# Column loops moved behind the first gathers in the projection and attention stages of a two-layer graph network

## The reference

```
h = relu(layernorm(x))
x = x + GCN(h):      h1 = batchnorm(h @ w1.T + b1); y = (relu(h1) @ w2.T + b2) @ w_gcn.T
                     deg = edges per dst, with one more self loop; dinv = deg ** -0.5
                     out[d] = sum over edges (y[s] * dinv[s]) * dinv[d] + b_gcn
h = relu(layernorm(x))
x = x + attention(h): q, k, v = h @ Wq + bq, h @ Wk + bk, h @ Wv + bv     (8 heads of 32)
                     s[e] = q[row] . k[col] * scale; softmax over the edges of each row
                     out[row] = (sum of a[e] * v[col]) @ Wo + bo
```

## Time and profile before

| what | value |
|---|---|
| median of 3 runs | 3371.53 us |
| the profiled execution's own time | 3372.14 us |
| its span, first to last instruction | 3370.4 us |
| busy: PE, DVE, ACT, POOL | 92%, 83%, 74%, 58% |
| granted TensorE clock, mean | 0.97 of full |
| end of the node stage's last DVE instruction | 1132.55 us |
| projection stage, first ACT instruction | 1132.84 us |
| projection stage, last ACT instruction | ends 2279.35 us |
| attention stage, first ACT instruction | 2282.27 us |

### The profile page before, as it was taken

The page is one execution under the profiler, slowest core; times in us unless marked ns, Lnnn a source line. Parts: engine busy times, 40 slices in busy tenths (PEclk is TensorE's granted clock), DMA queues, the critical chain, the costliest instruction groups (busy, mean ns, idle before and its releaser), DMA issues. The chain is left out here.

```text
span 3370.4 us, 80751 instructions
## 1 busy us (share of the span) xinstructions
PE 3093.8 (92%) x20244; PEld 2504.8 (74%) x20244; DVE 2804.0 (83%) x7375; ACT 2501.4 (74%) x7073; POOL 1953.4 (58%) x1668
## 2 busy tenths in 40 slices
PE   4899998899998399999999999994999999999999
PEld 2455554677776288888888888883999999999998
DVE  8888887778886478888888888885888888888887
ACT  3788887699997577777777777753777777777776
POOL 1155553255554387777777777754555555555553
PEclk7999999899999699999999999996999999999999
DMA  3455554788887578888888888865777777777774
GB/s 103 166 203 202 204 201 173 244 303 305 311 305 249 212 278 311 306 313 307 308 307 311 309 308 310 308 238 191 243 257 256 253 255 252 253 252 253 253 255 155
DMA packets 335634, 861.27 MB, mean 256 GB/s; under 512 B 98484, under 2 KB 152923, under 8 KB 323019
## 3 DMA queue, kind: packets, MB, share of 16 engines
q1 hardware_dynamic: 239178, 677.96, 56.4%
q0 software_dynamic: 66256, 78.94, 8.1%
q10 hardware_dynamic: 30128, 103.56, 7.7%
HBM read 521.95 MB, written 416.52 MB: 278 GB/s over the span
## 5 line engine op out<-in xcount | busy, mean ns | idle before, releaser
L1879 PE MATMUL c_qkv_ps<-w_qkv_hi,c_ht_hi 128*128 128x256 f16 x2352 | 642.3, 273 | 0.0
L1879 PE MATMUL c_qkv_ps<-w_qkv_lo,c_ht_hi 128*128 128x256 f16 x2352 | 642.3, 273 | 0.0
L1879 PE MATMUL c_qkv_ps<-w_qkv_hi,c_ht_lo 128*128 128x256 f16 x2352 | 642.2, 273 | 0.0
L2312 ACT ACTIVATE e_mine<-e_mine,e_attention 128x32 f32<-128x32 f32 x2352 | 518.7, 308 | 70.6 <-DVE e_attention L2546 70.6
L2259 POOL DMA_INDIRECT e_kv<-kv_table,e_near x392 | 401.7, 1025 | 113.4 <-issue 103.1
L1749 POOL DMA_INDIRECT c_got<-y_table,c_near x392 | 395.1, 1008 | 108.5 <-issue 97.5
L596 POOL DMA_INDIRECT dst_slots<-dst_word,dst_goal x240 | 241.4, 1006 | 302.7 <-ACT a_hn L660 237.5
L2348 PE MATMUL e_out_ps<-w_out,e_mean_t 128*128 128x256 f32 x1568 | 392.8, 380 | 0.0
L2251 POOL TENSOR_TENSOR e_kv<-e_kv,e_part_of 128x1024 f32<-128x1024 f32 x98 | 186.9, 1908 | 344.5 <-DVE e_part_of L2581 344.5
L722 PE MATMUL a_h_ps<-a_ht,w_t 128*128 128x512 f32 x784 | 363.1, 607 | 17.8 <-ACT h L642 14.1
L1513 POOL DMA_INDIRECT src_slots<-staged_word,staged_goal x240 | 234.9, 979 | 243.4 <-DVE sort_lane_hot L1402 170.9
(11 more groups left out here) (432 smaller groups left out, 7669.3 us busy)
## 6 DMA issues: line engine op xcount, KB each, us to landing
kv_table<-c_kv SPq DMA_DIRECT2D x98, 1024.0 KB
h_table<-h ACTq DMA_DIRECT2D x98, 512.0 KB, 2.7
h<-h_table SPq DMA_DIRECT2D x98, 512.0 KB, 4.1
y_table<-y_out ACTq DMA_DIRECT2D x98, 512.0 KB
agg_table<-agg_out SPq DMA_DIRECT2D x98, 512.0 KB
c_agg<-agg_table SPq DMA_DIRECT2D x98, 512.0 KB, 4.8
x_table<-c_x SPq DMA_DIRECT2D x98, 512.0 KB, 2.7
q_table<-c_q SPq DMA_DIRECT2D x98, 512.0 KB
```

Of the source, the lines that this page charges most:

```text
L1879: last = nc.tensor.matmul(qkv_ps[n][:, j * D:(j + 1) * D], h[u][:, kc, j * P:(j + 1) * P], wt[:, kc, n * D:(n + 1) * D], start=m == 0, sto ...
L2312: last = nc.scalar.activation(of_head, of_head, ACT.Copy, scale=attention[u][:, j, h, 0:1])
```

## The change

Six things, all in how stages start:

1. Projection stage: the column's word is decoded, and its gather issued, for turn 0 ahead of the loop; the loop body follows on each engine behind the first tiles' gathers (at the turn of the first sums), decodes the next word and issues the next gather at its end. `found` is one column wider for this. On POOL: gathers of tile 0, the column's gather, gathers of tile 1, the loop, gathers of tile 2.
2. SP no longer waits for the number of columns but for `sum_settled` (1 if nothing is unsorted), so the loads of `agg` start without the loop.
3. Gathers of the projection stage name partitions 0 to 126 only; POOL doesn't wait for the bias rows any more, each of the first four gathers waits for its own buffer's clearing, and SP's bias loads follow each clearing.
4. `absent` is made in the projection stage, on DVE, behind the sums of tile 1. `has_self` starts in the node stage, and `no_self` too, by a subtraction on POOL; POOL has no other `tensor_tensor` ahead of the projection stage.
5. Attention stage: the loop's first decoding stands at the end of the projection stage on DVE; on POOL the column's four gathers come first, then those of tiles 0, 1 and 2, then the loop's body with the scatters, the wait for them and four more gathers of a next column; on PE, ACT and DVE the body stands ahead of turn 1. SP copies to and from spare tiles behind the tables (`agg_spare`, `kv_spare`) when nothing is slow, doesn't wait for the columns then (`slow_settled`), and POOL doesn't wait for the second copy.
6. All six kv buffers are cleared by ACT, each ahead of its first index tile.

The core of the diff (the bodies of both loops are the same instructions as before, but for the decoding at their end):

```diff
+def is_first(t):
+    return t is not None and isinstance(t[0], int) and t[0] == 0 and t[1] == 0
...
-    agg_table = dram("agg_table", [TAB + 2 * P, D])
+    agg_spare = dram("agg_spare", [TAB + 2 * TILE, D])
+    agg_table = agg_spare[0:TAB + 2 * P, :]
-    kv_table = dram("kv_table", [TAB, 2 * D])
+    kv_spare = dram("kv_spare", [TAB + 2 * TILE, 2 * D])
+    kv_table = kv_spare[0:TAB, :]
...
+ v.tensor_scalar(has_self[:, :], n_self[:, :], 1.0, None, ALU.min).then_inc(has_ready, 1)
...
+ v.tensor_scalar(slow_last[:, :], slow[:, :], float(-2 * TILE), float((NT + 1) * TILE), ALU.mult, ALU.add)
- for l in range(LAYERS):
-     v.tensor_scalar(absent[:, :, l], own_degree[:, :], float(l), LOW, ALU.is_le, ALU.mult)
...
+ pool.wait_ge(has_ready, 1)
+ nc.gpsimd.tensor_tensor(no_self[:, :], has_self[:, :], one_col[:, 0:1].to_broadcast([P, NT * ROWS]), ALU.subtract)
...   (projection stage, SP)
- sp.wait_ge(got_cleared, 4)
  for w in four:
+     sp.wait_ge(got_cleared, w + 1)
- hold(sp, column_free, columns + 1)
+ hold(sp, column_free, settled)
...   (projection stage, POOL)
- with pool.Fori(0, columns) as n:
-     hold(pool, staged, n + 1)
-     gather(one_got[:, :], y_table, from_i[:, 0:1]).then_inc(gathered, 16)
-     hold(pool, summed_ready, n + 1)
-     hold(pool, goal_ready, n + 1)
-     scatter(agg_table, goal[:, 0:1], one_summed[:, :], compute_op=ALU.add).then_inc(scattered, 16)
-     hold(pool, scattered, n * 16 + 16)
-     pool.sem_inc(column_free, 1)
- pool.wait_ge(bias_rows, 64)
+ def add_columns():
+     with pool.Fori(0, columns) as n:
+         hold(pool, summed_ready, n + 1)
+         hold(pool, goal_ready, n + 1)
+         scatter(agg_table, goal[:, 0:1], one_summed[:, :], compute_op=ALU.add).then_inc(scattered, 16)
+         hold(pool, scattered, n * 16 + 16)
+         pool.sem_inc(column_free, 1)
+         hold(pool, staged, n + 2)
+         gather_column()
  def step(at):
+     if is_first(at(3)):
+         add_columns()
...
-     nc.gpsimd.indirect_dma_start(out=got[w][:, j, :], out_offset=None, in_=y_table,
-                                  in_offset=bass.IndirectOffsetOnAxis(ap=near[w][:, j:j + 1], axis=0),
+     nc.gpsimd.indirect_dma_start(out=got[w][0:P - 1, j, :], out_offset=None, in_=y_table,
+                                  in_offset=bass.IndirectOffsetOnAxis(ap=near[w][0:P - 1, j:j + 1], axis=0),
+     if is_first(at(1)):
+         pool.wait_ge(staged, 1)
+         gather_column()
...   (projection stage, DVE, end of a step, then end of the stage)
+ if at(3) is not None and isinstance(at(3)[0], int) and tile_of(at(3)) == 1:
+     for l in range(LAYERS):
+         v.tensor_scalar(absent[:, :, l], own_degree[:, :], float(l), LOW, ALU.is_le, ALU.mult)
  over_tiles(dve, plan, 9, step, slots=4)
+ decode_slow(dve, 0)
+ stage_slow()
...   (attention stage, SP)
- hold(sp, gathered, columns * 64)
  for t in range(SHORT):
      sp.dma_start(flat(q[t][:, :, :]), row_block(q_table, t)).then_inc(q_loaded[t], 16)
- hold(sp, column_free, columns + 1)
+ hold(sp, copied, tiles * 16)
+ hold(sp, column_free, settled)
- sp.sem_inc(rows_settled, 1)
...   (attention stage, POOL)
- pool.wait_ge(rows_settled, 1)
- pool.wait_ge(kv_cleared, RING)
+ pool.wait_ge(s_staged, 1)
+ gather_column()
...
+ if isinstance(t, int) and t < RING:
+     pool.wait_ge(kv_cleared, t + 1)
...
+ if is_first(at(0)):
+     settle_columns()
...   (attention stage, ACT, ahead of each of the first six index tiles)
+ if isinstance(t, int) and t < RING:
+     nc.scalar.activation(kv[w][:, :, :].rearrange("p r d -> p (r d)"), one_col[:, 0:1].to_broadcast([P, ROWS * 2 * D]),
+                          ACT.Copy, scale=0.0).then_inc(kv_cleared, 1)
```

More of the change, by code:

```diff
@@ L310, in build @@
         sum_cols = sb("sum_cols", [P, 1], I32, where=early)
+        sum_settled = sb("sum_settled", [P, 1], I32, where=early)
         sum_lane = sb("sum_lane", [P, NT * ROWS], where=early)
@@ L315, in build @@
         own_degree = sb("own_degree", [P, NT * ROWS], where=early)
+        has_self = sb("has_self", [P, NT * ROWS], where=early)
+        no_self = sb("no_self", [P, NT * ROWS], where=early)
         mid = ExitStack()
@@ L1483, in _ @@
                     v.tensor_copy(sum_cols[:, :], over[:, 3:4])
+                    v.tensor_scalar(sum_settled[:, :], over[:, 3:4], unsorted[:, 0:1], 1.0, ALU.mult, ALU.add)
                     v.tensor_scalar(sum_lane[:, :], slots_f[:, 0, :], neg_one[:, 0:1], float(P), ALU.mult, ALU.add)
@@ L1561, in build, with stage_slow @@
+        def stage_slow():
+            v = nc.vector
+            v.tensor_tensor(s_ends[:, 0:1], s_keys[:, 0:1], s_back[:, :], ALU.add)
+            v.tensor_copy(s_ends[:, 1:2], s_keys[:, 1:2]).then_inc(s_staged, 1)
         with ExitStack() as part, nc.Block() as block:
@@ L1609, in build @@
             state = [sb(f"c_state{u}", [P, ROWS, STATE], where=part) for u in two]
-            has_self = sb("has_self", [P, NT * ROWS], where=part)
-            no_self = sb("no_self", [P, NT * ROWS], where=part)
             got_cleared = sem("c_got_cleared")
@@ L1904, in _, with decode @@
                 v = nc.vector
-                with dve.Fori(0, columns) as n:
+                def decode(n):
                     steps = 8
@@ L1930, in _, with stage @@
                     link(v.scalar_tensor_tensor(node[:, :], odd[:, :], -254.0, node[:, :], ALU.mult, ALU.add))
+                    assert done[0] == steps
+                def stage(n):
+                    if not isinstance(n, int):
+                        hold(dve, gathered, n * 16)
                     v.scalar_tensor_tensor(from_i[:, :], node[:, :], parts[:, 1:2], live[:, :], ALU.add, ALU.mult).then_inc(staged, 1)
-                    assert done[0] == steps
-                    dve.wait_ge(across_ready, n + 1)
@@ L1941, in _, with rank_columns @@
-                    dve.wait_ge(ranked, n * 2 + 2)
-                    v.tensor_scalar(goal[:, :], apart[:, :], spare[:, 2:3], None, ALU.add).then_inc(goal_ready, 1)
-                v.tensor_scalar(has_self[:, :], n_self[:, :], 1.0, None, ALU.min).then_inc(c_chain, 1)
-                dve.wait_ge(c_chain, 1)
-                v.tensor_scalar(no_self[:, :], has_self[:, :], -1.0, -LOW, ALU.add, ALU.mult).then_inc(c_chain, 1)
-                dve.wait_ge(c_chain, 2)
+                def rank_columns():
+                    with dve.Fori(0, columns) as n:
+                        dve.wait_ge(across_ready, n + 1)
+                        v.tensor_scalar(same[:, :], across[:, 0:P], key[:, 0:1], None, ALU.is_equal)
+                        v.scalar_tensor_tensor(rank_of[:, :], across[:, 0:P], key[:, 0:1], earlier[:, :], ALU.is_equal, ALU.mult,
+                                               accum_out=rank[:, 0:1])
+                        v.tensor_scalar(apart[:, :], key[:, :], spare[:, 2:3], None, ALU.subtract).then_inc(ranked, 1)
+                        dve.wait_ge(ranked, n * 2 + 1)
+                        v.scalar_tensor_tensor(apart[:, :], rank[:, :], 0.0, apart[:, :], ALU.is_equal, ALU.mult).then_inc(ranked, 1)
+                        dve.wait_ge(ranked, n * 2 + 2)
+                        hold(dve, column_free, n + 1)
+                        v.tensor_scalar(goal[:, :], apart[:, :], spare[:, 2:3], None, ALU.add).then_inc(goal_ready, 1)
+                        dve.wait_ge(goal_ready, n + 1)
+                        decode(n + 1)
+                        stage(n + 1)
@@ L1948, in _ @@
+                decode(0)
+                stage(0)
+                v.tensor_scalar(no_self[:, :], no_self[:, :], -LOW, None, ALU.mult).then_inc(c_chain, 1)
                 v.tensor_scalar(has_self[:, :], has_self[:, :], SCALE, None, ALU.mult).then_inc(c_chain, 1)
```

315 lines of the change are left out of this document (169 added, 146 removed).

## The result

| | before | after |
|---|---|---|
| median (runs) | 3370.6 us (4) | 3853.9 us (4), 3852.8 to 3855.3 |
| ratio, 95% interval | | 1.1435 [1.1421, 1.1448] |
| span of the profiled execution | 3370.4 us | 3851.0 us |
| projection stage, first ACT instruction to that of the attention stage | 1149.4 us | 1644.1 us (1129.45 to 2773.51) |
| attention stage, from there to the end | 1088.1 us | 1077.5 us |

The account below looks back on a forecast made before the run. PE was taken to bound both long stages once filled, so only their starts could gain: 11.7 us in the projection stage plus 14.4 in the attention stage, 26.1 off 3372.1, giving 3346.0 us, range 3337 to 3361.

Parts of the forecast that it names:

- Steady loop, "I take 0": Projection loop: 98 times four gathers go from 128 to 127 partitions, bytes stay, so the time changes by 0.
- The second rival: Projection loop: a 127-row gather costs more than one of 128; 66 us more, 3412; chance 0.14, 0.10 beyond 0.2% slower.
- landing of 16 us: Second rival's threshold: gathers of 127 rows decide from a landing of about 16 us, or 0.27 us more of issue.
- Node stage's end, -0.6: End of the node stage: with the masks gone the last store sets the end, 0.6 us gained, bounded by 0 and 3.3.
- Projection stage, POOL's load: POOL's 6.8 us gap before tile 0's addition is a one-time load, moved to the node stage; addition 15.7 us earlier.
- Projection stage, DVE: Start of the projection stage: the 7.15 us of masks aren't hidden, normalising starts 11.7 us earlier, the 0.6 included.
- Attention stage, -14.4: Start of the attention stage: 14.4 us gained, set by POOL's first weighting of v; bounds -17.3 and -10.
- DVE's line: Attention stage's start: DVE reaches tile 0's products at 2308.8 instead of 2326.08, 17.3 us earlier.
- POOL's: Attention stage's start: POOL's first weighting of v, behind scatter and gathers, at 2329.6 instead of 2340.60, 11.0 us earlier.
- Rival 3: Projection stage: the change doesn't remove POOL's 6.8 us load; the stage gains 8.9 instead of 11.7, 3349; chance 0.10.
- rival 1: Stage starts: the loop's wait in POOL's queue and early transfers lose 5 us more per stage, 3356; chance 0.14.

Follow-up runs that it names:

- experiment 5: The kernel of experiment 4 without POOL's subtraction in the node stage (DVE makes `no_self` at the projection stage's start): 3404.0 us, 0.9956, beside 3400.3 of its base.
- experiment 4: The changed kernel with the projection stage's gathers naming all 128 partitions again and the masks back in the node stage: 3349.1 us, 0.9930 of the kernel before.
- experiment 6: On experiment 4's kernel (3400.3 us there): POOL weighs v two turns earlier, 3389.9; column's gather ahead of tile 0's, 3394.5; both, 3387.0 us.

## Why the prediction was wrong, step by step

- **Steady loop, "I take 0".** This is the step that failed. I argued that bytes stay, and they nearly do; the price is POOL's time per gather, 1.6 us more, 6.4 a tile. POOL had 1.3 of them to spare (1.08 by the one row I read), and 5.1 are left. The second rival named mechanism, place and threshold ("0.27 us more of issue"), and got 0.10 beyond 0.2%. I sized it by 0.7 us a tile; the measured 5.1 over 98 tiles are 500. Its landing of 16 us played no part (10.8 measured), and by its own terms, 22.2 less 5.2, it should have read 17. No gather of other than 128 rows stood in the trace, so the range for this cost should have stayed open upward; instead I let what the rows didn't show argue for nothing.
- **Node stage's end, -0.6.** Not told: it began 3.4 us earlier in the changed trace, but between two kernels that differ only by the masks it moved by 3.3 the other way (1134.85 without them there, 1131.59 with). That stage varies by more than the term.
- **Projection stage, POOL's load.** Right: gap gone, found in the node stage, back in experiment 5. First `c_got` 2.5 us behind the start, as said.
- **Projection stage, DVE.** The masks do stand in the path; to have them there costs 5.7 us net where the sum had 3.4. With 128 rows `c_stats` gains 4.4 us (38.8 against 43.2 before), of a forecast 11.1, and the first product comes 54.2 us behind the start, not 47 (48.8 in experiment 4). Of the missing 6.7 us, 4.4 are lost before the masks start (29.4 behind the stage's start, forecast 24.9), 2.1 of them by the wait for the bias row that all 128 rows need (first gather 4.65 us behind the start, not 2.54), and 1.8 by the column's landing, since PE's column sum came 6.9 us behind its gather (1145.10 to 1152.02), not 5.1. The other 2.3 are the masks, lengthened by POOL's addition beside them.
- **Attention stage, -14.4.** 10.6 in the changed kernel, 12.0 in the one of experiment 4 (3347.4 - 2271.32 against 1088.1). DVE's line was forecast at 26.5 us behind the start and is at 26.4; POOL's at 47.3 and is at 50.0, at 47.9 in experiment 4. That POOL is the later is shown by PE's wait of 9.58 us for it, and by experiment 6.
- **Rivals 1 and 3.** Rival 3 is refuted. Losses near the 5 us a stage of rival 1 are there, 6.7 and 2.4 to 3.8 us. Most of the first is the bias row (2.1) and the masks (2.3); the 1.8 of the column's later landing are of the kind that the rival named, though no run tests what delays it.
- With 128 rows the change comes to 3354.8 and 3349.1, both inside the range; with 127 the range was no use.

## What to carry to other kernels

A gather by indirect DMA is priced on POOL by how its row count divides: keep 128 rows, or 120 or 112, and let a skipped index or a table row do what a shorter slice would. When an edit sits in a loop of 98 turns and no row of the trace shows its new form, bound it by the engine's spare time per turn and measure that form alone first. And undo parts one by one: the parts that looked harmless behind the slow gathers (the masks) cost 6 us once these were gone.

## Not expected of the hardware

- One gather of 127 rows of 1 KB: 528 packets and 2.59 us of POOL; of 128: 48 and 1.00; of 126: 64 and 1.05.
- A DVE `tensor_scalar` into bf16 with a stride of 8 holds an indirect DMA's issue until it ends (6.44 and 5.23 us for 1.0); the flat f32 one doesn't. A POOL addition of 2.36 us made the one mask beside it 3.79 us long, where they are 1.3.
- The kernel before took 3372 us in one group of runs and 3419 to 3421 in three. By the traces 8.5 us of it are ahead of the projection stage (start at 1141.33 against 1132.84), 30.5 in it (1179.9 us against 1149.4) and 7.7 behind. With 125 rows its loop took 11.1 us a tile in one of these three groups. The cause wasn't found.
